# Decoder stack on one core: the layer norm behind the second self-attention taken in groups of four batches, partly inside the attention's loop

## What is computed

```python
x = x + _L0_attn_ref(_layernorm(x), ...)              # gated linear attention + GELU feed-forward
x = x + _L0_xattn_ref(_layernorm(x), ctx_1024, ...)   # cross-attention, 16 heads of 64
x = x + _L0_ffn_ref(_layernorm(x), ...)               # block-wise fake-quantized linear layer
x = x + _L1_attn_ref(_layernorm(x), ...)              # causal self-attention, 16 heads of 16
x = x + _L1_xattn_ref(_layernorm(x), ctx_1024, ctx_1024, ..., mask_BxS2_ik1)   # one head of 256
x = x + _L1_ffn_ref(_layernorm(x), ...)               # gated feed-forward, quantized activations

def _layernorm(x, axis=-1, eps=1e-05):
    m = jnp.mean(x, axis=axis, keepdims=True)
    v = jnp.var(x, axis=axis, keepdims=True)
    return (x - m) / jnp.sqrt(v + eps)
```

## Time and profile before

| | |
|---|---|
| time, median of 3 runs | 1420.88 us (1418.55 to 1423.24) |
| the profiled execution | 1413.2 us, of which the span is 1411.4 us |
| PE busy / DVE / ACT / POOL over the span | 89% / 72% / 53% / 17% |
| PE's mean granted clock, share of full speed | 0.958 |
| the self-attention loop | about 1010 to 1150 us from the span's start |
| norm and transposes behind it | 1150 to 1160 us |
| slots of the cross-attention | from 1160 us |

### The profile page before, as it was taken

How to read it: one execution, slowest core, us unless ns; L and a number is a source line. 1 busy time by engine, 2 the same in 40 slices (tenths; PEclk the granted TensorE clock), 3 DMA queues, 4 the chain that set the end, 5 groups by cost and what they waited for, 6 DMA issues and landing times.

```text
span 1411.4 us, 27724 instructions
## 1 busy us (share of the span) xinstructions
PE 1258.5 (89%) x9826; PEld 1071.0 (76%) x9826; DVE 1015.6 (72%) x2558; ACT 750.8 (53%) x1833; POOL 245.6 (17%) x330
## 2 busy tenths in 40 slices
PE   5999999979999999999999999999799969979219
PEld 4899989868778877778787777877577757869218
DVE  5975777455677778777777777777688865756974
ACT  5653535354655656555556655555356644426472
POOL 2333334233000000000000000000144433200100
PEclk9999999989999999999999999999889989989659
DMA  9201010041000000000000000000100022200001
GB/s 279 69 1 35 12 30 16 19 145 36 12 4 9 12 12 11 11 11 0 11 11 11 11 11 0 11 1 1 46 15 3 2 69 88 88 0 1 0 0 47
DMA packets 34548, 40.67 MB, mean 29 GB/s; under 512 B 4889, under 2 KB 29066, under 8 KB 34442
## 3 DMA queue, kind: packets, MB, share of 16 engines
q1 hardware_dynamic: 33614, 39.24, 9.2%
q10 hardware_dynamic: 828, 0.14, 0.1%
HBM read 35.36 MB, written 4.01 MB: 28 GB/s over the span
## 4 chain that ended last, share of the span: by engine, by line
PE 54%; DVE 15%; issue 5%; ACT 4%; POOL 1%; DVEq 0%; ACTq 0%; POOLq 0%
PE bank L780 9%; PE bank L782 8%; PE bank L781 8%; PE bank L985 4%; PE bank L1001 4%; PE bank L993 3%; PE bank L961 3%; ACT prob L1671 2%; DVE amax L2502 2%; DVE nmx L2312 2%; PE bank L1234 2%; PE bank L1252 2%; PE bank L1357 2%; PE bank L1319 1%; DVE kTl L2084 1%
## 5 line engine op out<-in xcount | busy, mean ns | idle before, releaser
L1671 ACT ACTIVATE prob<-bank,nmx 100x361 f32<-100x361 f32 x256 | 142.5, 559 | 156.8 <-DVE nmx L2312 155.9
L2312 DVE TENSOR_REDUCE nmx<-bank 100x1 f32<-100x361 f32 x256 | 124.2, 527 | 22.7 <-PE bank L985 15.7
L695 POOL TENSOR_TENSOR frstd<-fmoments,eps 100x1 f32<-100x1 f32 x32 | 6.2, 193 | 646.5 <-DVE fmoments L2255 646.4
L780 PE MATMUL bank<-cxTh,wxkh 128*128 128x362 f32 x256 | 99.9, 390 | 3.9 <-DVE kTl L2084 2.8
L1001 PEld LDWEIGHTS bank<-pT,vv 128*64 128x64 f32 (+1 forms) x1536 | 70.8, 138 | 37.4 <-issue 27.1
L1001 PE MATMUL bank<-pT,vv 128*64 128x100 f32 (+1 forms) x1536 | 96.1, 260 | 2.0 <-DVE oTl L2083 2.0
L2329 DVE TENSOR_SCALAR prob<-prob,rsum 100x361 f32<-100x361 f32 x256 | 92.9, 405 | 4.5
L1657 ACT CAST oTh<-bank 128x100 fp32r<-128x100 f32 x128 | 31.8, 248 | 112.3 <-PE bank L1001 112.1
L993 PE MATMUL bank<-ident,prob 100*128 100x100 f32 (+1 forms) x768 | 90.1, 253 | 1.5 <-DVE prob L2329 1.5
L2083 DVE TENSOR_TENSOR oTl<-bank,oTh 128x100 fp32r<-128x100 f32 x128 | 32.9, 257 | 80.1 <-ACT oTh L1657 76.8
L993 PEld LDWEIGHTS bank<-ident,prob 100*128 100x128 f32 (+1 forms) x768 | 84.9, 152 | 7.1 <-DVE prob L2329 2.6
(11 more groups left out here) (427 smaller groups left out, 3708.6 us busy)
## 6 DMA issues: line engine op xcount, KB each, us to landing
cx<-in_ctx_dram SPq DMA_DIRECT2D x32, 128.0 KB, 2.1
xc<-in_ctx_dram SPq DMA_DIRECT2D x32, 128.0 KB
parked_weights<-parking SPq DMA_DIRECT2D x9, 256.0 KB, 5.5
mask_i<-in_mask_BxS_ik_dram SPq DMA_DIRECT2D x16, 141.0 KB
w<-in_L_attn_W_dram SPq DMA_DIRECT2D x2, 1024.0 KB, 14.2
cx<-in_ctx_dram SPq DMA_DIRECT2D x16, 105.0 KB, 2.0
xc<-in_ctx_dram SPq DMA_DIRECT2D x16, 105.0 KB
x<-in_x_dram SPq DMA_DIRECT2D x4, 400.0 KB
```

Source lines behind the costliest of these rows:

```text
L780: pe.matmul(o, wh, mh, start=start, stop=False)
L1671: nc.scalar.activation(prob[:, h % 4, :], bank[S_BANKS[e]][0:T, 0:S], ACT.Exp, bias=nmx[:, h:h + 1], accum_out=psum_[:, h:h + 1]).then_inc ...
L2312: nc.vector.tensor_reduce(nmx[:, h:h + 1], bank[S_BANKS[e]][0:T, 0:S], AX_X, ALU.max, negate=True).then_inc(xa_max, 1)
```

## The change

Four things move, and nothing is computed with another formula but rstd, which becomes (var + eps) to the power -0.5 on POOL instead of a square root on ACT and a reciprocal on DVE.

1. **Statistics by group in the loop.** At the end of DVE's iteration 5, 9 and 13 the four aggregations of group 0, 1, 2 (`group_moments`), behind a wait for DVE's own last statistics. POOL then takes rstd of the group (`group_deviation`, two instructions over four columns, behind its subtractions for batch 6, 10, 14), and DVE in iteration 6, 10, 14 computes -mean * rstd (`minus_means`). Group 3 follows at the loop's end: three aggregations before `heads_scaled(15)`, the fourth behind the last statistics.
2. **Rows by ACT.** z = rstd * x + (-mean * rstd) for groups 0 to 2 is one ACT instruction a batch (`half_normalised`), in halves of two: behind the exponentials in iterations 7 and 8, 11 and 12, and behind the last copies of iteration 15.
3. **Transposes and copies.** PE transposes group 0 ahead of `heads_weighted(15)` (banks 0, 1), group 1 behind it (banks 2, 3), group 2 behind `heads_output(15)` (banks 4, 5). ACT copies them behind its last rows.
4. **Group 3 in the next stage.** DVE normalises its four batches in the first slot, behind the context copy; PE transposes them in the second slot, behind the context transposes (banks 2, 3); ACT copies them there, ahead of the first exponentials. The wait for x of the last batch moves on PE from ahead of the transposes to the second slot.

The diff, cut to its core:

```diff
@@ -419,6 +419,7 @@
     PAIRS = B // 2
+    N2_BANKS = (0, 2, 4, 2)
@@ -451,7 +452,7 @@
-    TURN = {1: 2 * NG + 4, 2: 2 * NG + 5, 3: 2 * NG + 6}
+    TURN = {1: 2 * NG + 4}
@@ -701,6 +702,18 @@
+        def group_deviation(g):
+            nonlocal links
+            links += 1
+            rows = slice(G * g, G * g + G)
+            pool.wait_ge(var_ready, TURN[1] + 2 * g + 1)
+            nc.gpsimd.tensor_tensor(rstd_all[:, rows], moments_all[:, rows, 1], eps[0:T, :].broadcast_to([T, G]),
+                                    ALU.add).then_inc(pool_link, 1)
+            pool.wait_ge(pool_link, links)
+            nc.gpsimd.tensor_tensor(rstd_all[:, rows], rstd_all[:, rows], minus_half[0:T, :].broadcast_to([T, G]),
+                                    ALU.pow).then_inc(std_ready, 1)
@@ -722,7 +735,10 @@
+            if b > 5 and b % G == 2:
+                group_deviation((b - 6) // G)
+        group_deviation(NG - 1)
         pool.wait_ge(a1_x, B)
@@ -762,18 +778,14 @@
-        def all_transposes(n):
-            for g in range(NG):
-                pe.wait_ge(ln_z, NG * (n - 1) + g + 1)
-                if g >= 2:
-                    pe.wait_ge(ln_done, KD * NG * (n - 1) + KD * (g - 1))
-                for k in range(KD):
-                    for t in range(G):
-                        mm = pe.transpose(bank[KD * (g % 2) + k][:, t * T:(t + 1) * T],
-                                          z[:, G * g + t, k * P:(k + 1) * P], ident[0:T, 0:T])
-                    mm.then_inc(ln_t, 1)
-            pe.wait_ge(ln_done, KD * NG * n)
+        def rows_transposed(g):
+            pe.wait_ge(ln_z, NG + g + 1)
+            for k in range(KD):
+                for t in range(G):
+                    mm = pe.transpose(bank[N2_BANKS[g] + k][:, t * T:(t + 1) * T],
+                                      z[:, G * g + t, k * P:(k + 1) * P], ident[0:T, 0:T])
+                mm.then_inc(ln_t, 1)
@@ -1297,18 +1309,24 @@
                 queries_projected(b // 2 + 1)
+            if b == B - 1:
+                pe.wait_ge(a1_sum, 4 * B)
+                rows_transposed(0)
             heads_weighted(b)
...
                 values_projected(b + 2)
+        rows_transposed(1)
         heads_output(B - 1)
-        pe.wait_ge(a1_x, B)
-        all_transposes(2)
+        rows_transposed(2)
+        pe.wait_ge(ln_done, KD * NG + 2 * KD)
...
             there, c, o = step(1)
+            if isinstance(g, int) and g == 0 and r == 1:
+                pe.wait_ge(ln_done, KD * NG + 3 * KD)
+                pe.wait_ge(a1_x, B)
             if there:
@@ -1329,6 +1347,8 @@
             if there and r == 0:
+                if not isinstance(g, int):
+                    pe.wait_ge(ln_done, 2 * KD * NG)
                 for m in range(KD):
@@ -1340,6 +1360,8 @@
                     mm.then_inc(x1_t, 1)
+            if isinstance(g, int) and g == 0 and r == 1:
+                rows_transposed(NG - 1)
             there, c, o = step(3)
@@ -1439,10 +1461,6 @@
-        def all_deviations(turn):
-            act.wait_ge(var_ready, turn)
-            nc.scalar.activation(std_all[:], moments_all[:, :, 1], ACT.Sqrt, bias=eps[0:T, :]).then_inc(std_ready, 1)
@@ -1460,12 +1478,11 @@
-        def all_copies(n, turn):
-            all_deviations(turn)
-            for g in range(NG):
-                for k in range(KD):
-                    act.wait_ge(ln_t, KD * NG * (n - 1) + KD * g + k + 1)
-                    rows_out(g, k, KD * (g % 2) + k)
+        def rows_copied_2(g):
+            for k in range(KD):
+                act.wait_ge(ln_t, KD * NG + KD * g + k + 1)
+                rows_out(g, k, N2_BANKS[g] + k)
@@ -1769,6 +1786,16 @@
+        def half_normalised(g, half):
+            if half == 0:
+                act.wait_ge(var_ready, TURN[1] + 2 * g + 2)
+            for b in range(G * g + 2 * half, G * g + 2 * half + 2):
+                ins = nc.scalar.activation(z[:, b, :], x[:, b, :], ACT.Identity, scale=rstd_all[:, b:b + 1],
+                                           bias=std_all[:, b:b + 1])
+            if half:
+                ins.then_inc(ln_z, 1)
@@ -1788,8 +1815,14 @@
-        all_copies(2, TURN[2])
+            if b > 6 and b % G == 3:
+                half_normalised((b - 7) // G, 0)
+            if b > 6 and b % G == 0:
+                half_normalised((b - 8) // G, 1)
+        half_normalised(NG - 2, 1)
+        for g in range(NG - 1):
+            rows_copied_2(g)
@@ -1808,6 +1841,8 @@
                 nc.scalar.copy(xcT[:, o, 0, :], bank[0][:, 0:S]).then_inc(x1_ca, 1)
+            if isinstance(g, int) and g == 0 and r == 1:
+                rows_copied_2(NG - 1)
             there, c, o = step(1)
@@ -1907,33 +1942,29 @@
-        def all_rows(turn, src=None):
-            if src is None:
-                link(nc.vector.memset(pause[:, 3:4], 0.0))
-            else:
-                for b in range(B):
-                    ins = nc.vector.bn_stats(stats_all[:, b, :], src[:, b, :])
-                link(ins)
-            for b in range(B):
+        def row_of(tensor, g, t):
+            return tensor[:, ds(G * g + t, 1), :].rearrange("p a d -> p (a d)")
+        def group_moments(g, first, last):
+            for b in range(G * g + first, G * g + last):
                 ins = nc.vector.bn_aggr(moments_all[:, b, :], stats_all[:, b, :])
-            ins.then_inc(var_ready, 1)
-            dve.wait_ge(std_ready, turn)
-            link(nc.vector.reciprocal(rstd_all[:], std_all[:]))
-        def all_normalized(group):
-            for b in range(G * group, G * group + G):
+            return ins
+        def minus_means(g):
+            rows = slice(G * g, G * g + G)
+            dve.wait_ge(std_ready, TURN[1] + g + 1)
+            nc.vector.scalar_tensor_tensor(std_all[:, rows], moments_all[:, rows, 0], -1.0, rstd_all[:, rows], ALU.mult,
+                                           ALU.mult).then_inc(var_ready, 1)
+        def group_normalised(g, first, last):
+            dve.wait_ge(std_ready, TURN[1] + g + 1)
+            for b in range(G * g + first, G * g + last):
...
-        def row_of(tensor, g, t):
-            return tensor[:, ds(G * g + t, 1), :].rearrange("p a d -> p (a d)")
-        def norm(n, src=None):
-            all_rows(TURN[n], src)
-            for g in range(NG):
-                all_normalized(g).then_inc(ln_z, 1)
@@ -2442,12 +2473,18 @@
             if b:
-                row_stats_1(b - 1)
+                ins = row_stats_1(b - 1)
+            if b > 4 and b % G == 1:
+                link(ins)
+                group_moments((b - 5) // G, 0, G).then_inc(var_ready, 1)
+            if b > 5 and b % G == 2:
+                minus_means((b - 6) // G)
+        link(ins)
+        group_moments(NG - 1, 0, G - 1)
         heads_scaled(B - 1)
         outputs_added(B - 1)
-        row_stats_1(B - 1)
-        norm(2)
+        link(row_stats_1(B - 1))
+        group_moments(NG - 1, G - 1, G).then_inc(var_ready, 1)
@@ -2473,6 +2510,8 @@
                 nc.vector.tensor_copy(xcT[:, o, 1, :], bank[1][:, 0:S]).then_inc(x1_cd, 1)
+            if isinstance(g, int) and g == 0 and r == 0:
+                group_normalised(NG - 1, 0, G).then_inc(ln_z, 1)
             there, c, o = step(3)
```

## The result

The changed kernel takes 1406.8 us in the median of four runs (1404.6 to 1407.3), the kernel before 1419.7 in four runs beside it (1416.1 to 1423.2). The ratio is 0.9915, with a 95% interval of 0.9896 to 0.9935. In two later comparisons with five rounds each the ratio was 0.9927 [0.9912, 0.9941] and 0.9924 [0.9907, 0.9941], which is 10.4 and 10.8 us less. Between the medians the three differences are 12.9, 12.1 and 10.6 us. All times are of fast runs; two slow runs of the kernel before, 1508.8 and 3063.0 us in the second comparison, are left out.

The account below looks back on a forecast made before the run. PE was taken to bound the loop's end, waiting for batch 15's norm, then transposing. Removing that, less added DVE, ACT and transpose work, at full clock, gave 9.3 us less: 1420.9 to 1411.6 us, range 1408 to 1416.5.

Parts of the forecast that it names:

- DVE's statistics: DVE, end of the loop: aggregations and the small mean product put 0.5 us on the path (0.3 to 0.8).
- The full clock around 1150: PE, loop's end: filled waits keep 2.4 GHz, so the last output product takes about 0.95 us instead of 2.03.
- A: Rival, PE at the loop's end: the clock falls all the same, costing 2.9 us; gain 6.4, time 1414.5; chance 0.14.
- B: Rival, the loop: it pays in full for ACT's and DVE's added work; gain 4.7, time 1416.2; chance 0.12.
- C: Rival, next stage: slots wait for POOL's stretched splits; at three times their length 1428.9 us, slower than before; chance 0.03.
- D: Rival, second slot: group 3 doesn't fit; missed altogether it costs about 1.5 us, time 1413.1; chance 0.09.
- ACT 0.1: ACT's normalised rows in the loop: mostly absorbed, 0.1 us on the path; 3.6 if nothing were hidden.
- group 0 0.2 us: PE's transposes of group 0, 0.85 us in its 0.63 us wait for ACT: 0.2 us on the path.
- Group 2: PE's eight transposes of group 2 behind the last output product: 0.85 us on the path.
- Removed from the path: PE, between batch 15's output product and the next stage's first product: 9.83 us of waiting and transposing goes.
- How the numbers follow: Chances for the whole kernel: forecast as summed 0.60; faster by over 4.3 us 0.86, slower 0.03, within 0.11.
- POOL's cover: Next stage's slots: 2.5 us remain between POOL's late first rstd and DVE's row maximum, so nothing is lost.

Follow-up runs that it names:

- nofill: Changed kernel with PE's transposes of groups 0 and 1 moved behind the last output product, out of PE's waits; 1410.0 us, ratio 0.9935 to the kernel before.
- rows_twice: Changed kernel with each ACT row of groups 0 and 1 computed a second time into unread memory; 1408.3 us, ratio 0.9937 to the kernel before.
- b_again: The kernel before, unchanged, profiled and timed once more over five rounds; 1419.1 us, ratio 1.0004 to the runs beside the first result.

## Why the prediction was right, and where it fell short

**What went as told.** The removed stretch: all of it left the path, and the mechanism is the one forecast. DVE's statistics: the last output product is 0.54 us later than before (forecast 0.5 for DVE alone). The full clock around 1150, the hidden group 1, the fit of group 3 on DVE (0.42 us to spare, forecast 0.3), the loop unchanged up to batch 12, DVE's row maximum not waiting for POOL. Rivals A, B, C and D did not happen; nofill shows A's price when the filling is missing (1.8 us by the clock, against 2.9 reckoned), rows_twice shows how far B was.

**A reading that held for one profile only.** That transposes keep the clock up was argued from its rise while PE did nothing but transposes. In the two later profiles of before it did not rise during them. The forecast of full clock came true, but not on the strength of that row; what bears it out is nofill against the changed kernel.

**Terms mis-sized in the sum, together 0.4 us.** ACT 0.1 and group 0 0.2 us were put on the path and cost nothing measurable: the last output product stands at 1148.81 with the shift taken off, where the sum without these two gives 1148.77. Group 2 adds 0.69 us (1153.06 to 1153.75), not 0.85: the row's length overlaps with the product behind it, so the spacing of rows was the right reading. With these the first product comes at 1150.44 instead of 1150.87, and the gain against the first profile is 9.7 us at that point and 9.8 in the third slot.

**The step that failed: the kernel before was taken from one execution.** "Removed from the path" priced what lay between the output product and the first product, by one profile, and left the first product itself at 2.95 us on both sides. That was right for that execution. In the two other profiles of before that product runs at half clock for most of its length (4.37 and 4.59 us), and the change removes that too: the stretch is 11.0 and 11.1 us shorter, where the sum had 9.3. The price was in the prediction, "the first product partly at half clock, about 1.5 us", but only as a loss that the changed kernel might have (rival A), not as one that the kernel before may have, as two of its three profiles do. The earlier trace rows showed the half clock lasting until 1158, 2 us before the first product's start.

**"How the numbers follow".** The difference was carried to 1420.9 us, the median of three runs between 1418.6 and 1423.2. The profiled execution itself, at 1413.2, lay 5 us under the lowest of them, which should have been read as: an execution with few clock falls. The traces bear that out: over the first 315 us its mean granted clock is 0.98, in all twelve others 0.95 to 0.97. Later medians of before were 1419.7, 1419.1, 1417.8 and 1417.8 (4, 19, 13 and 11 runs). With 1419.1 and 1417.8, the two beside the repeats of the changed kernel, the summed 9.3 us would give 1409.8 and 1408.5, and the measured 11.0 us 1408.1 and 1406.8, against 1407.0 and 1407.2 of the changed kernel on these chips. So the 4.8 us between forecast and result are some 1.8 us of gain that the sum didn't see, and the rest, 3 us, is base and chance: against 1419.7, the four runs beside the result, the base was 1.2 us too high, and the difference of 12.9 us in that comparison is 1.8 more than any pair of traces shows at the loop's end. Where these 1.8 come from isn't shown; they are within the interval of that ratio. The lower end allowed for 10.2 us of gain and 2.7 of scatter; it had to allow for 11.1 and, with three runs for a base, for about 3.

**What scatters.** The table of stretches shows it: 0 to 1500 takes 300.9 to 306.6 us, 6600 to 6900 either 41.5 or 43.2 to 44.0, in both kernels, with the same instructions. The window over the second of these in the first profile of before:

```profile
962.00:1022.00 60.00, 49.53 (x408) 38.44 (x406) 39.33 (x121) 28.47 (x93) 5.80 (x15) 0.91 0.08 21
```

And in the second profile (b_again):

```profile
963.00:1023.00 60.00, 51.95 (x410) 40.51 (x408) 37.48 (x116) 28.56 (x93) 5.78 (x15) 0.86 0.05 15
```

Nearly the same work (408 and 410 matmuls), in a window shifted by 1 us, took PE 2.4 us longer at a mean granted clock of 0.86 instead of 0.91.

**What stays open.** What decides in an execution when exactly the clock falls isn't told by these traces. The profiles don't say how often the kernel before has the short loop's end of 35.4 us; one of three had. The stretch 9130 to 9300 took 38.0 to 38.9 us in four profiles of kernels with the change, and 39.3 to 39.6 in all three of before but also in the other six with it; from 9000 to the last matmul the same four took 195.2 to 196.4 us and all others 197.1 to 197.5. Whether the change makes the short form possible or these are chances, three profiles of before can't tell. Up to 2.4 us hang on it.

**POOL's cover** was forecast at 2.5 us and is 1.4. The weights landed 0.6 us later than the shifted profile of before says (1164.56, against 1160.61 + 3.31 = 1163.92), and the slots are 0.4 us earlier. Neither reached the path.

## What to carry to other kernels

A norm behind a loop needs the last batch for the last group only: the groups before it go into the loop and into the waits at its end, and the last group into the next stage's first idle time, which alone was worth some 7 us here. Work put into a matmul engine's waits pays twice, by itself and by the clock that doesn't fall; whoever costs the removal of a wait reads on, behind it, until the clock is full again, in more than one execution of the kernel before. A base for a forecast is a median of many runs, and a profile that is quicker than all timed runs is no typical one.

## What the runs showed of the hardware

Eight transposes in each of two waits, 0.63 and 1.93 us long, were enough to hold the granted clock at 1.00; without them it was at 0.79 in the 2 us window in which the wait of 1.93 us ended, at 0.50 in the next, and the work behind ran 1.8 us longer. The clock's fall can be early or late around the same wait: in one execution the product right behind it took 2.03 us, in two others 1.11 and 1.20, with the loss (4.59 and 4.37 us instead of 2.95) in a product that starts 11.6 and 11.7 us later. In these two 32 transposes in a row, 5.57 us, went by at half clock. A wait of 2.13 us of PE's in a later slot also brought the clock down (2.38 us for 1.38 us of work). Two table loads on ACT took 1.28 us each, and the activation behind started 0.01 us after the load's end.
